# Attention scores with the keys on partitions, and row sums by a product with ones, in an attention and GRU kernel

## The chip, the core and the metric

The kernel runs on one core of one Trainium2 chip. The metric is the device time of one execution in microseconds (us). Engines: TensorE (PE, whose weight loads are listed apart as PEld), VectorE (DVE), ScalarE (ACT), GpSimd (POOL), and SyncE (SP), which here issues nearly all transfers. Data that engines share lies in SBUF; PE writes to PSUM, which has 8 banks of 512 float32 numbers on each of 128 partitions.

## The reference

`x` is 16 batches of 256 rows of 512; 16 heads of 32; all float32. A first layer is attention, a second a GRU that walks the 256 rows of all batches together.

```
xn = rms_norm(x) * g_norm * (1 + scale) + shift          # scale, shift: cond @ W_emb + b_emb
q, k, v = split(xn @ W_qkv)                               # each 16 heads of 32
q, k = rms_norm(q) * g_q, rms_norm(k) * g_k               # over the 32 numbers of a head
attn = softmax(q @ k.T * 32 ** -0.5)                      # 256 x 256, for each head and batch
o = attn @ v
x = x + o + o @ W_out
# GRU over the 256 rows, h starts as cond
r, z = sigmoid(i_r + h_r), sigmoid(i_z + h_z)             # i = x_t @ W_ih + b_ih, h_ = h @ W_hh + b_hh
n = tanh(i_n + r * h_n);  h = (1 - z) * n + z * h
out[:, t] = x[:, t] + h
```

## The kernel before

**Stages.** The attention stage goes over the 16 batches and lasts until 666.6 us; the GRU's 256 steps follow, its first step at 672.7 us. Each engine has its own program, written out by hand, and they meet at semaphores (`wait_ge`, `then_inc`). The engines take their instructions in the order of the program.

**A pass.** The attention stage has 64 passes, p = 0 to 63, four to a batch (b = p // 4, v = p % 4). A pass handles 8 heads for 128 queries. `scores(p + 1)` (L572) makes eight products of 32 x 128 by 32 x 256 with the queries on the output's partitions, in four row groups at a time. `maxima` (DVE, L872) takes the row maxima, negated, in two reductions of 1024 numbers for each partition. `exps` (ACT, L1237) takes eight exponentials of 256 numbers with the maximum as bias and collects the row sums beside them. `turn_p` (PE, L591) turns the probabilities, eight 128 x 128 transposes for each half of the pass; `keep_turned_p` copies them out of PSUM, half on ACT (L1252) and half on DVE (L887). `times_v` (L606) multiplies by v, sixteen products with 32 output rows and 128 columns. `recips` and `turn_recips` (L976, L980, L614) turn the row sums' reciprocals, `scale` (L892) applies them, `high` and `low` split the result in a rounded part and a rest for the output product.

**Filling.** Between these stand the large products, each of twelve 128 x 128 by 128 x 512 instructions (x and weights each split in a rounded part and a rest, three terms): six `project` products for a batch's q, k and v (L512) and two `out_proj` products (L627). The function `slots(p)` says which stands where: two in each pass. Piece `("project", b, i, g)` is rows 128 i to 128 i + 127 of batch b, g = 0 for q, 1 for k, 2 for v.

**Preparing q and k.** Each q or k product is copied to SBUF (`keep_raw`), squared (`square_raw`), both on ACT, summed by heads (`squares`, DVE L820), raised to the power -0.5 on POOL (`rsqrt`, L1427 and L1431) and multiplied (`normalize`, DVE L827). k and the second half of q then go out to DRAM and back in another layout, and DVE turns them in 32 x 32 blocks (`turn_k` L837, `turn_q` L846); the first half of q is turned on PE (`turn`, L551) inside a large product. `scale_q` (ACT, L1223) applies g_q, g_k and the scale. For the batch after, x is loaded in blocks; `square_blocks` (ACT, L1153), `x_sums` (DVE, L792), `sums` (PE, L705), `x_mean` (DVE) and `scale_blocks` (POOL, L1411 and L1414) norm it; `turn_x`, `affine` (DVE, L803, L811), `x_high` (ACT, L1164) and `x_low` (POOL, L1422) make the operands of its products.

## Time and profile before

| | |
|---|---|
| median of 3 runs | 1676.29 us (1675.59 to 1678.32) |
| the profiled execution | 1676.52 us, of it the span of the trace 1674.7 us |
| attention stage, by its last `times_v` | until 666.6 us |
| first GRU step on PE | 672.7 us |
| one batch of the attention stage (middle) | 39.84 us |
| PE busy in 294 to 372 us | 78.00 of 78.00 us |
| DVE, ACT, POOL busy there | 63.64, 59.27, 35.99 us |

In the rows below, a matmul in float32 is listed as two instructions and one in float32r (a rounded float32) as one; a transpose is one.

### The profile page before, as it was taken

How to read it: one execution, taken by the hardware profiler on the slowest of the kernel's cores; microseconds unless marked ns; L12 is line 12 of the kernel's file. 1: busy time of each engine (PE TensorE's matmuls, PEld its weight loads, DVE VectorE, ACT ScalarE, POOL GpSimd, SP SyncE). 2: the span in 40 equal slices, each digit the busy share in tenths (PEclk: the TensorE clock that was granted, in tenths of full speed). 3: DMA queues.
4: the chain of work that ended last, by engine and by line, in shares of the span. 5: the costliest groups of instructions: out<-in, count | busy, mean ns of one | idle time of the engine just before them, and what ended most of it. 6: DMA issues, size and time to landing. Idle time of an engine off the chain costs nothing.

```text
span 1674.7 us, 71812 instructions
## 1 busy us (share of the span) xinstructions
PE 1658.6 (99%) x30549; PEld 1292.1 (77%) x30549; DVE 1194.5 (71%) x4267; ACT 933.4 (56%) x3139; POOL 409.3 (24%) x464
## 2 busy tenths in 40 slices
PE   9999999999999999999999999999999999999998
PEld 7787777888788887777777777777777777777776
DVE  6888878888888876666666666666666666666665
ACT  5777777777777776444444444444444444444443
POOL 4544444444444430011111111111111111111111
PEclk9999999999999999999999999999999999999999
DMA  6244443333344426211111111111111111111110
GB/s 202 57 118 124 115 100 89 89 96 96 96 97 102 94 76 149 44 30 25 31 30 27 28 30 27 30 29 27 32 28 27 32 29 26 32 29 26 31 25 16
DMA packets 234280, 100.02 MB, mean 60 GB/s; under 512 B 141196, under 2 KB 213720, under 8 KB 233960
## 3 DMA queue, kind: packets, MB, share of 16 engines
q1 hardware_dynamic: 233840, 95.40, 23.0%
q8 instruction: 240, 3.93, 1.0%
q14 instruction: 80, 0.66, 0.1%
q10 hardware_dynamic: 120, 0.04, 0.0%
HBM read 58.38 MB, written 36.96 MB: 57 GB/s over the span
## 4 chain that ended last, share of the span: by engine, by line
PE 95%; DVE 1%; ACT 1%; POOL 1%; SPq 1%; issue 1%; DMA 1%; DVEq 0%; ACTq 0%; POOLq 0%
PE ps L763 40%; PE ps L649 20%; PE ps L512 14%; PE ps L591 7%; PE ps L627 5%; PE ps L572 4%; PE ps L606 3%; PE ps L614 1%; POOL rq L1431 1%; SPq L285 0%; PE ps L551 0%; ACT P L1237 0%; PE ps L533 0%; DVE nmx L872 0%; PE ps L541 0%
## 5 line engine op out<-in xcount | busy, mean ns | idle before, releaser
L649 PE MATMUL ps<-wih,x1T 128*32 128x192 f32 x8192 | 379.6, 326 | 0.3 <-issue 0.3
L1373 ACT ACTIVATE v<-ps 128x128 f32<-128x128 f32 x512 | 140.7, 275 | 414.6 <-PE ps L763 414.6
L763 PE MATMUL ps<-whh,hTE 128*32 128x192 f32 x8192 | 356.3, 326 | 1.1 <-DVE hTE L1102 1.1
L763 PE MATMUL ps<-whh,hTO 128*32 128x192 f32 x8192 | 356.3, 326 | 0.0
L1486 POOL TENSOR_TENSOR outG<-hG,x1g 128x128 f32<-128x128 f32 x255 | 116.3, 456 | 920.4 <-DVE hG L1095 920.4
L649 PEld LDWEIGHTS ps<-wih,x1T 128*32 128x32 f32 x8192 | 266.5, 110 | 66.7 <-issue 0.6
L763 PEld LDWEIGHTS ps<-whh,hTE 128*32 128x32 f32 x8192 | 249.8, 110 | 84.3 <-DVE hTE L1102 15.5
L763 PEld LDWEIGHTS ps<-whh,hTO 128*32 128x32 f32 x8192 | 250.0, 110 | 83.0 <-issue 0.4
L1075 DVE SCALAR_TENSOR_TENSOR v<-v,ps 128x64 f32<-128x64 f32 x512 | 113.4, 222 | 237.5 <-ACT v L1373 237.5
L1237 ACT ACTIVATE P<-ps,nmx 128x256 f32<-128x256 f32 x496 | 229.7, 483 | 0.3 <-DVE nmx L872 0.3
L1381 ACT ACTIVATE v<-v 128x64 f32<-128x64 f32 x512 | 131.5, 257 | 132.5 <-DVE v L1080 132.5
L1431 POOL TENSOR_TENSOR rq<-msq,mh 128x16 f32<-128x16 f32 x64 | 185.9, 2905 | 5.3
L872 DVE TENSOR_REDUCE nmx<-ps 128x4 f32<-128x1024 f32 x128 | 156.0, 1219 | 18.1 <-PE ps L572 18.0
L1091 DVE TENSOR_TENSOR v<-v,v 128x64 f32<-128x64 f32 x512 | 115.7, 226 | 63.6 <-ACT v L1381 48.1
L512 PE MATMUL ps<-wqh,xh 128*128 128x512 f32 x360 | 151.5, 421 | 1.5 <-ACT xt L1192 1.5
L512 PE MATMUL ps<-wql,xh 128*128 128x512 f32 x360 | 141.6, 393 | 0.0
L1377 ACT ACTIVATE v<-v 128x64 f32<-128x64 f32 x512 | 131.6, 257 | 16.1
L512 PE MATMUL ps<-wqh,xl 128*128 128x512 f32 x360 | 140.5, 390 | 0.0
L591 PE MATMUL ps<-ident,P 128*128 128x128 f32 x1024 | 138.5, 277 | 1.0 <-DVE rTs L892 0.7
L591 PEld LDWEIGHTS ps<-ident,P 128*128 128x128 f32 x1024 | 114.1, 142 | 30.7 <-issue 20.8
L1252 ACT COPY PT<-ps 128x512 f32<-128x512 f32 x128 | 74.3, 581 | 92.9 <-PE ps L591 92.9
L1095 DVE SCALAR_TENSOR_TENSOR hG<-v,v 128x64 f32<-128x64 f32 x512 | 114.3, 223 | 8.8
(139 smaller groups left out, 2155.5 us busy)
## 6 DMA issues: line engine op xcount, KB each, us to landing
xres<-in_x_dram SPq DMA_DIRECT2D x32, 256.0 KB, 3.4
...
xblk<-x1s SPq DMA_DIRECT2D x128, 64.0 KB, 2.7
x1g<-xscr SPq DMA_DIRECT2D x128, 64.0 KB, 2.0
...
```

The source lines that it names most:

```text
L512: last = pe.matmul(pB, xp[e2][:, c, m], wp[:, c, n], start=(k == 0), stop=(k == 3 * KC - 1))
L591: last = pe.transpose(pP[:, j, k, :], P[:, U % 4, j, 128 * k:128 * k + 128], ident)
L649: last = pe.matmul(gb[pr % 2][q][32 * j:32 * j + 32, 64:256], x1T[:, tt % 2, r, c, :], wig[:, c, :, 128 * j + 64 * q:128 * j + 64 * q + 64 ...
L763: last = pe.matmul(gb[e][q][32 * j:32 * j + 32, 0:192], h[:, c, :], whg[:, c, :, 128 * j + 64 * q:128 * j + 64 * q + 64], start=False, sto ...
L872: done = v.tensor_reduce(nmx[:, p % 2, j, :], ps[:, j, :].rearrange("p j (e t) -> p j e t", e=2), AXX, ALU.max, negate=True)
L1091: v.tensor_tensor(v_n[:, q, :], v_n[:, q, :], v_c[:, q, :], ALU.mult).then_inc(s_d, 1)
L1237: last = s.activation(P[:, (2 * p + e) % 4, j, :], pS[e][:, j, :], ACT.Exp, scale=rq0[:, 4 * (2 * p + e) + j:4 * (2 * p + e) + j + 1] if p ...
L1373: s.activation(v_rz[:, q, :], gb[e][q][:, 64:192], ACT.Tanh, scale=0.5).then_inc(s_tr, 1)
L1377: s.activation(v_c[:, q, :], v_rz[:, q, 64:128], ACT.Copy, bias=0.5, scale=-0.5)
L1381: s.activation(v_n[:, q, :], v_w[:, q, :], ACT.Tanh).then_inc(s_n, 1)
L1431: g_.tensor_tensor(rq0 if k == 2 else rq[:, i, :], msq[:, i, :], mh, ALU.pow).then_inc(s_rq, 1)
L1486: g_.tensor_tensor(outG[:, tt % 2, k, :], hG[:, t % 2, :], x1g[tt % 2][:, k // 2, :], ALU.add).then_inc(s_og, 1)
```

## The change

A pass becomes a group G, again 64, four to a batch (w = G % 4), but of four heads for all 256 queries. In the diff and in what follows, n = b + 1 and m = b + 2.

- Rounded copies of q and k (`qTr`, `kTr`, float32r) are made once for a batch by two new copies of 1024 numbers on ACT (`round_q`, `round_k`). `first_scores` makes the scores of these copies with queries on partitions, only to take the row maxima.
- The maxima are turned on PE (`turn_maxima`, two transposes), copied out on ACT (`keep_maxima`), and brought into the real scores by a product with a 0/1 matrix (`SEL`, four instructions of 512 columns). The real `scores` have the keys on partitions and are added to it in the same PSUM banks 0 to 3.
- `exps` is now two exponentials of 1024 numbers without bias or sums, and its output needs no turning: `turn_p` and `keep_turned_p` go (16 transposes, two copies on ACT and two on DVE for each pass).
- Row sums: DVE adds the two key tiles (`add_tiles`, two of 512 numbers), PE multiplies the sum by ones (`row_sums`), DVE turns, inverts and turns back (`recips`, 256 and 8 and 256 numbers) and scales.
- `high` moves from DVE to ACT, `low` from DVE to POOL.
- `slots(G)` puts the large products in another order, `turn_maxima(G + 1)` inside the first of a group's two, behind 8 of its 12 instructions. The q turn stands within the second one of w = 1, likewise.
- At the start, q of batch 0 is normed and turned in full before the first scores. The second half of `wih` is loaded only near the end of the attention stage, since its place is taken until then.

```
+def slots(G):
...
+    if w == 3:
+        return [("project", m, 0, 1), ("project", m, 1, 1)] if m < NB else [None, None]
+    if w == 0 and n < NB:
+        return [("project", n, 1, 0), ("project", n, 0, 0)]
+    if w == 1 and n < NB:
+        return [("project", n, 0, 2), ("project", n, 1, 2)]
+    if b and w == (2 if n < NB else 0):
+        return [("out", b - 1, 0), ("out", b - 1, 1)]
+    return [None, None]
+def within(G):
+    b, w = G // 4, G % 4
+    return ("turn", b + 1, 0, 0) if w == 1 and b + 1 < NB else None
+def behind(G):
+    b, w = G // 4, G % 4
+    return ("sums", b + 2) if w == 0 and b + 2 < NB else None
+PASS = {5: [], 6: [("project", 0, 1, 0)], 7: [("rows", 1, 0)]}
+for _G in range(-1, NP):
+    for _k, _x in enumerate(slots(_G)):
+        if _x:
+            PASS[6 + _k].append(_x)
+    PASS[5] += [_x for _x in (("maxima", _G + 1) if _G + 1 < NP else None, behind(_G), within(_G)) if _x]
+for _i in range(2):
+    PASS[6 + _i].append(("out", NB - 1, _i))
...
+            load_x1()
+            sp.wait_ge(s_S1, NP)
+            emptied(sp, ("out", NB - 2, 1))
+            load_wih(1)
...
+                    if k == 8 and between:
...
+            def first_scores(G):
+                b, c = G // 4, G % 4
+                if c == 0:
+                    pe.wait_ge(s_qr, 2 * b + 2)
+                if G:
+                    pe.wait_ge(s_ex, 2 * G)
+                for i in range(2):
                     for j in range(4):
                         q = slice(32 * j, 32 * j + 32)
...
+                        last = pe.matmul(ps[:, j, 256 * i:256 * i + 256], qTr[q, i, c, :], kTr[q, c, :], start=True, stop=True)
+                last.then_inc(s_S1, 1)
+            def turn_maxima(G):
+                bank_free(("maxima", G))
+                pe.wait_ge(s_mx, 2 * G + 2)
+                for i in range(2):
+                    last = pe.transpose(ps[:, 5, 128 * i:128 * i + 128], nmx[:, i, :], ident)
+                last.then_inc(s_nT, 1)
+            def scores(G):
+                b, c = G // 4, G % 4
+                emptied(pe, ("maxima", G))
+                if G == 0:
+                    pe.wait_ge(s_sel, 3)
+                for j in range(4):
+                    q = slice(32 * j, 32 * j + 32)
+                    pe.matmul(ps[:, j, :], SEL[q, :], nmT[q, :].unsqueeze(1).to_broadcast([32, 2, 256]), start=True, stop=False,
+                              skip_group_check=True)
+                for k in range(2):
+                    for j in range(4):
+                        q = slice(32 * j, 32 * j + 32)
+                        last = pe.matmul(ps[:, j, 256 * k:256 * k + 256], kT[b % 2][q, c, 128 * k:128 * k + 128], qT[b % 2][q, :, c, :],
+                                         start=False, stop=(k == 1), skip_group_check=True)
...
+                for k in range(2):
+                    for j in range(4):
+                        h = 4 * c + j
+                        pe.matmul(pO[32 * j:32 * j + 32, :], V[:, b % 2, k, 32 * h:32 * h + 32], PT[:, G % 2, k, j, :],
+                                  start=(k == 0), stop=(k == 1))
+            def row_sums(G):
+                pe.wait_ge(s_ps, 2 * G + 2)
+                for j in range(4):
+                    last = pe.matmul(pR[32 * j:32 * j + 32, :], ones, PS[:, j, :], start=True, stop=True)
...
-            def turn_recips(p):
-                bank_free(("recips", p))
-                pe.wait_ge(s_rb, p + 1)
-                for e in range(2):
-                    last = pe.transpose(pR[:, 128 * e:128 * e + 128], rB[:, e, :], ident)
-                last.then_inc(s_rT, 1)
...
+            def group(G):
+                first, second = slots(G)
+                if G + 1 < NP:
+                    first_scores(G + 1)
+                if G >= 0:
+                    times_v(G)
+                    row_sums(G)
+                fill(first, (lambda: turn_maxima(G + 1)) if G + 1 < NP else None)
+                if G + 1 < NP:
+                    scores(G + 1)
+                if behind(G):
+                    passed(behind(G))
+                inner = within(G)
+                fill(second, inner and (lambda: passed(inner)))
+            for G in range(-1, NP):
...
+                    v.wait_ge(s_sel, 3)
+                v.tensor_reduce(nm4[:, j, :], ps[:, j, :].rearrange("p j (i t) -> p j i t", i=2), AXX, ALU.max,
+                                negate=True).then_inc(s_mx, 1)
+            def add_tiles(G, h):
+                j = slice(2 * h, 2 * h + 2)
+                v.wait_ge(s_ex, 2 * G + h + 1)
+                if G:
+                    v.wait_ge(s_pv, G)
+                v.tensor_tensor(PS[:, j, :], PT[:, G % 2, 0, j, :], PT[:, G % 2, 1, j, :], ALU.add).then_inc(s_ps, 1)
+            def recips(G):
+                v.wait_ge(s_pv, G + 1)
+                v.transpose(rA, pR).then_inc(s_rt, 1)
+                v.wait_ge(s_rt, G + 1)
+                v.reciprocal(rinv, rA.rearrange("p (u k) -> p u k", k=32)[:, :, 0]).then_inc(s_ri, 1)
+                if G >= 2:
+                    v.wait_ge(s_ol, G - 1)
+                v.wait_ge(s_ri, G + 1)
...
+                add_tiles(G, 0)
+                add_tiles(G, 1)
+                if G + 1 < NP:
+                    maxima(G + 1, 0)
+                    maxima(G + 1, 1)
+                if w == 0 and n < NB:
...
+                    normalize(n, 0, 1)
+                elif w == 1 and n < NB:
+                    squares(n, 0, 0)
+                    normalize(n, 1, 0)
+                elif w == 3 and b and n < NB:
+                    out_sum(b - 1, 1)
+                recips(G)
+                scale(G)
+                if w == 0 and n < NB:
+                    if m < NB:
+                        x_sums(m)
                     normalize(n, 1, 1)
...
+                    squares(n, 1, 0)
+                    if m < NB:
+                        x_mean(m)
+                elif w == 1 and n < NB:
+                    normalize(n, 0, 0)
                     turn_k(n)
...
+                    if m < NB:
+                        turn_x(m)
+                        affine(m, 0)
+                elif w == 2 and n < NB:
+                    if m < NB:
+                        affine(m, 1)
+                    turn_q(n)
+                    if b:
...
+            def round_q(n):
+                if n:
+                    s.wait_ge(s_q1, n)
+                    emptied(s, ("turn", n, 0, 0))
+                    s.wait_ge(s_S1, 4 * n)
+                else:
+                    s.wait_ge(s_qk0[0], 2)
+                s.copy(qTr, qT[n % 2]).then_inc(s_qr, 1)
+            def keep_maxima(G):
+                s.wait_ge(s_nT, G + 1)
+                s.copy(nmT, ps[:, 5, 0:256]).then_inc(s_ev[5], 1)
+            def exps(G, h):
+                j = slice(2 * h, 2 * h + 2)
+                s.wait_ge(s_S, G + 1)
+                if G >= 2:
+                    s.wait_ge(s_pv, G - 1)
+                s.activation(PT[:, G % 2, :, j, :], ps[:, j, :].rearrange("p j (k t) -> p k j t", k=2), ACT.Exp).then_inc(s_ex, 1)
+            def high(G):
...
+                keep(slots(G - 1)[1])
+                if G:
+                    high(G - 1)
                 if w == 0 and m < NB:
                     square_blocks(m)
...
+                if w == 2 and n < NB:
+                    keep_turned_q(n, 0)
+                    scale_q(n)
+                    round_q(n)
+                    if m < NB:
+                        x_high(m, 0)
+                if G + 1 < NP:
+                    keep_maxima(G + 1)
+                keep(slots(G)[0])
+                if w == 2 and n < NB:
+                    round_k(n)
+                    if m < NB:
                         x_high(m, 1)
...
+                if G + 1 < NP:
+                    exps(G + 1, 0)
+                    exps(G + 1, 1)
...
+            def low(G):
+                b, c = G // 4, G % 4
+                e = (b + 1) % 2
+                g_.wait_ge(s_oh, G + 1)
+                g_.tensor_tensor(ol[e][:, c, :], oS[:, G % 2, :], oh[e][:, c, :].bitcast(F32), ALU.subtract).then_inc(s_ol, 1)
...
+                if G:
+                    low(G - 1)
+                if w == 0 and n < NB:
+                    rsqrt(n, 1, 1)
+                    rsqrt(n, 1, 0)
+                    if m < NB:
+                        scale_blocks(m)
+                elif w == 1 and n < NB:
+                    rsqrt(n, 0, 0)
+                elif w == 2 and m < NB:
                     x_low(m, 0)
                     x_low(m, 1)
+                elif w == 3 and m < NB:
+                    rsqrt(m, 0, 1)
```

On PE this is one group (w = 1) now, from `first_scores` to `scores`, with the last third of the first large product between:

```order
L561 MATMUL ps<-kTr,qTr 128x256 x8
L601 MATMUL ps<-PT,V 32x256 x8
L608 MATMUL ps<-PS,ones 32x256 x4
...
L512 MATMUL ps<-wqh,xl_90 128x512
L568 MATMUL ps<-ident,nmx 128x128 x2
L512 MATMUL ps<-wql,xh_88 128x512
...
L579 MATMUL ps<-nmT,SEL 128x512 x4
L584 MATMUL ps<-qT_84,kT_86 128x256 x8
L512 MATMUL ps<-wqh,xh_88 128x512
```

The scores' products L584 now stand behind the maxima of the same group, and no transposes of P are left.

On ACT, at the end of a pass with v = 0 in the kernel before: `scale_q` (L1223, its input turned by DVE) stood behind the exponentials (L1237).

```order
L1237 ACTIVATE P,rsum<-ps,nmx 128x256 x4
L1192 COPY xt<-ps 128x4x4x32
L1211 ACTIVATE sq<-xt 128x512
L1252 COPY PT<-ps 128x512
L1237 ACTIVATE P,rsum<-ps,nmx 128x256 x4
L1223 ACTIVATE qT_85<-xt,gqs 128x512
L1192 COPY xt<-ps 128x4x4x32
```

On ACT now, a group with w = 2, between the exponentials of one group and of the next (both L1218):

```order
L1218 ACTIVATE PT<-ps 128x2x512 x2
L1188 COPY V<-ps 128x512
L1225 CAST oh<-oS 128x256
L1175 ACTIVATE qT_83<-ps,gqs 128x512
L1180 ACTIVATE qT_83<-kx,gqs 128x512
L1207 CAST qTr<-qT_83 128x1024
L1122 CAST xh_89<-xf 128x512
L1211 CAST nmT<-ps 128x256
L1197 CAST kTr<-kT_85 128x1024
L1122 CAST xh_89<-xf_105 128x512
L1218 ACTIVATE PT<-ps 128x2x512 x2
```

`scale_q` (L1180), `round_q` (L1207) and `x_high` (L1122) now stand ahead of `keep_maxima` (L1211), and on DVE `turn_q` (L843), which `scale_q` waits for, stands in the same group behind `maxima`, `recips`, `scale` and `affine`.

On POOL in the kernel before, from a batch's second `rsqrt` (two instructions each) over `scale_blocks` (L1411, L1414) to its third:

```order
L1427 TENSOR_SCALAR msq<-ssq 128x16
L1431 TENSOR_TENSOR rq<-msq,mh 128x16
L1411 TENSOR_TENSOR rxp<-msp,mh 128x8
L1414 TENSOR_TENSOR xb<-xb,rxp 128x1024
L1427 TENSOR_SCALAR msq<-ssq 128x16
L1431 TENSOR_TENSOR rq<-msq,mh 128x16
```

On POOL now, from the last `rsqrt` of w = 0 (L1400, L1404) to the one of w = 1:

```order
L1400 TENSOR_SCALAR msq<-ssq 128x16
L1404 TENSOR_TENSOR rq<-msq,mh 128x16
L1383 TENSOR_TENSOR rxp<-msp,mh 128x8
L1386 TENSOR_TENSOR xb<-xb,rxp 128x1024
L1410 TENSOR_TENSOR ol_82<-oS,oh_73 128x256
L1400 TENSOR_SCALAR msq<-ssq 128x16
L1404 TENSOR_TENSOR rq<-msq,mh 128x16
```

The `rsqrt` ahead of `scale_blocks` was that of k's second half; now it is that of q's second half, whose product stands in the same group, and `low` (L1410) has come between.

## Rows read from the trace of the kernel before

**Rows 1.** The page's parts 1 and 2: busy us by engine; the clock granted to PE.
```profile
PE 1658.6 (99%) x30549; PEld 1292.1 (77%) x30549; DVE 1194.5 (71%) x4267; ACT 933.4 (56%) x3139; POOL 409.3 (24%) x464
...
PEclk9999999999999999999999999999999999999999
```
**Rows 2.** Busy us (and instructions) of PE, PEld, DVE, ACT, POOL, clock, DMA.
```profile
294.00:372.00 78.00, 78.00 (x721) 62.39 (x719) 63.64 (x110) 59.27 (x181) 35.99 (x23) 1.00 0.39 96
```
**Rows 3.** The chain that ended last, in order of time: start us, us, what.
```profile
290.35 1.01 PE ps L606 x32
...
320.39 1.01 PE ps L606 x32
321.40 1.08 PE ps L572 x16
322.48 1.02 PE ps L591 x8
...
323.72 2.77 PE ps L512 x12
326.49 0.87 PE ps L591 x8
327.36 2.82 PE ps L512 x12
330.19 1.01 PE ps L606 x32
```
**Rows 4.** The same chain where the GRU begins.
```profile
661.23 3.65 DMA x1n<-x1s
...
672.67 2.74 PE ps L763 x64
```
**Rows 5.** DVE's instructions in order of time: start us, us, what, [idle before <-releaser].
```profile
312.74 1.23 DVE L872 TENSOR_REDUCE nmx<-ps 128x4 f32<-128x1024 f32 x1 [0.58 <-PE ps L572]
313.88 0.68 DVE L887 COPY PT<-ps 128x512 f32<-128x512 f32 x1
314.48 0.68 DVE L827 TENSOR_TENSOR raw<-raw,rq 128x512 f32<-128x512 f32 x1
315.08 1.22 DVE L872 TENSOR_REDUCE nmx<-ps 128x4 f32<-128x1024 f32 x1
```
**Rows 6.** DVE groups by line: count, busy us, mean ns of one, idle before.
```profile
L846 DVE STREAM_TRANSPOSE xt<-raw 128x512 f32<-128x512 f32 x15 | 10.6, 706 | 2.7 <-DMA raw<-qscr 2.7
L892 DVE TENSOR_TENSOR rTs<-ps,rTs 128x256 f32<-128x256 f32 x64 | 26.9, 420 | 16.5 <-PE ps L606 16.5
L811 DVE TENSOR_SCALAR xf<-xt,Aff,Shf 128x256 f32<-128x256 f32 x56 | 20.4, 407 | 0.0
L976 DVE RECIPROCAL rinv<-rsum 128x8 f32<-128x8 f32 x64 | 12.4, 193 | 37.8 <-ACT P L1237 37.8
```
**Rows 7.** ACT groups by line, the same columns.
```profile
L1237 ACT ACTIVATE P<-ps,nmx 128x256 f32<-128x256 f32 x496 | 229.7, 483 | 0.3 <-DVE nmx L872 0.3
...
L1246 ACT COPY rTs<-ps 128x256 f32<-128x256 f32 x64 | 23.9, 373 | 5.6 <-PE ps L614 1.5
L1164 ACT CAST xh<-xf 128x512 fp32r<-128x512 f32 x30 | 18.9, 633 | 10.1 <-DVE xf L811 10.1
L1153 ACT ACTIVATE sqx<-xb 128x1024 f32<-128x1024 f32 x14 | 14.9, 1065 | 12.3 <-DMA xb<-in_x_dram 12.3
L1223 ACT ACTIVATE qT<-xt,gqs 128x512 f32<-128x512 f32 x15 | 11.1, 743 | 0.0
```
**Rows 8.** POOL groups by line, the same columns.
```profile
L1431 POOL TENSOR_TENSOR rq<-msq,mh 128x16 f32<-128x16 f32 x64 | 185.9, 2905 | 5.3
L1422 POOL TENSOR_TENSOR xl<-xf,xh 128x512 fp32r<-128x512 f32 x29 | 37.0, 1277 | 95.6 <-ACT xh L1164 86.9 <-ACT xh L1168 8.7
L1414 POOL TENSOR_TENSOR xb<-xb,rxp 128x1024 f32<-128x1024 f32 x14 | 26.7, 1909 | 1.1
L1411 POOL TENSOR_TENSOR rxp<-msp,mh 128x8 f32<-128x8 f32 x14 | 22.9, 1637 | 21.9 <-DVE msp L798 21.9
```
**Rows 9.** PE's instructions in order of time at the start, the first two scores.
```profile
31.51 1.15 PE L572 MATMUL ps<-kT,qT 32*128 32x256 f32 x16 [0.78 <-DVE kT L831]
...
39.44 1.15 PE L572 MATMUL ps<-kT,qT 32*128 32x256 f32 x16
```
**Rows 10.** DMA issues: engine, kind, count, KB each, median us to landing.
```profile
wih<-in_L_cond_W_ih_dram SPq DMA_DIRECT2D x3, 1024.0 KB, 6.0
```

606 lines of the change are left out of this document (209 added, 397 removed).

## The prediction, made before the changed kernel was run

> **What bounds the kernel now.** I read the page's busy shares first: PE is busy 99% of the span and the clock granted to it is full in every slice [rows 1]. The GRU stage is not touched but for its start, so the attention stage is read alone: in 78 us of its middle PE is busy for all 78.00 us, DVE for 63.64 [rows 2]. Then the chain that ended last: it runs on PE without a gap, one pass from 320.39 to 330.19 us, four passes from 290.35 to 330.19, which is 39.84 us for a batch [rows 3]. A pass is bound by the work on PE: work taken from PE is gained in full, as long as PE still never waits. So there are two questions: how much PE work is left, and whether the new order makes it wait.
>
> **PE's work.** Of a pass go the transposes of P, 1.02 + 0.87 us, those of the reciprocals (about 0.2, what is left of 9.80 after the other rows), and `times_v` in its old shape, 1.01 [rows 3]. What comes:
> - `first_scores`: eight instructions. The old scores, 16 instructions, took 1.08 us, 0.067 each [rows 3]; so 0.54. Bounds: 0.27, if one pass over the columns in float32r is half of a float32 instruction's; 0.87, if they follow each other like the eight transposes [rows 3]. The value taken is that of the same shape.
> - `turn_maxima`: two transposes, a quarter of 0.87, 0.22.
> - the selector product: four instructions of 512 columns. Twelve such take 2.77, 0.23 each [rows 3], so 0.92 one after another, 0.23 if four row groups run at a time as in the scores; taken 0.28.
> - the real scores: 1.08 as before, the same shape.
> - `times_v` and `row_sums`: 16 and 8 instructions with 32 output rows and 256 columns. The GRU's, with 192 columns, take 2.74 for 64, 0.043 each [rows 4], so 0.057 here: 0.91 and 0.46.
> - two large products, 2.81 and 2.80.
>
> A group is 9.10 us. With the q turn (four transposes, 0.44) and `sums` (0.1) a batch is 37.0 us against 39.84: **PE has 2.9 us less work for each batch**, if it never waits. Bounds of the unknown ones together: 8.8 to 10.1 for a group.
>
> **The chain through a group.** Now I follow the waits, since four engines hand to each other: `first_scores(G + 1)` needs the banks that the exponentials of G read, `maxima` follow, `turn_maxima`, `keep_maxima` on ACT, the scores, the exponentials. Durations for the others: on DVE the next instruction starts 1.14 us after a reduction of 1024 numbers and 0.60 after an operation on 512, DVE starts 0.06 behind PE [rows 5]; so two maxima are 2.36. `recips` and `scale`: a turn of 512 is 0.71, an operation on 256 is 0.42 [rows 6]; I take 0.44 for each turn of 256, 0.19 for the reciprocal, 0.42 for `scale`, 0.1 at each of three waits in between, in all 1.7. On ACT [rows 7]: 0.37 for `keep_maxima` and `high`; 1.06 for a copy of 1024; 0.63 for 512; 0.74 for `scale_q`; exponentials of 1024: 0.48 for 256 plus 768 further at the slope of the two copies (0.26 for 256) make 1.25, against 1.06 for a square; I take 1.1, 2.15 for both. On POOL [rows 8]: an `rsqrt` 2.9 + 0.3, `scale_blocks` 1.64 + 1.91, `low` half of 1.28.
>
> Times in each group from its first instruction on PE:
> - *w = 3.* `first_scores` to 0.54, maxima 0.60 to 2.96; PE has `times_v`, `row_sums` and eight instructions of the large product until 3.79, turns the maxima until 4.01; `keep_maxima` until 4.43, under the rest of the product (4.94). Scores to 6.30, exponentials to 8.5, second product to 9.10. PE never waits: 9.1 us.
> - *w = 0.* DVE goes on from 2.9 with `squares`, `normalize` (0.6 each) and `recips`, `scale` to 5.8, then `x_sums` to 6.95. `sums` on PE stands ahead of the second product and waits for it, from 6.30 to 7.1: 10.0 us. DVE then norms k's second half and sums q's second half (8.2). Its `rsqrt` ends at 11.5, `scale_blocks` at 15.1, both on POOL.
> - *w = 1*, from 10.0. POOL is busy with that until 5.1, `low` until 5.8, and only then takes the `rsqrt` of q's first half: 9.05. `normalize` ends at 9.75. The q turn on PE, in the second product, would be due at 8.2: it starts at 9.9, and the group takes 11.3 us. Behind it DVE has `turn_k`, `turn_x` (as a reduction of 1024, 1.16 each), two `affine` (0.41 each), so 12.8, and the next `add_tiles` 14.0, 2.7 us into the next group.
> - *w = 2*, from 11.3. `row_sums` wait for that (3.3), the maxima end at 5.1. DVE: `recips`, `scale` 6.7, `affine` 7.4, `turn_q` 8.1. ACT has waited for `turn_q`: `scale_q` 8.9, `round_q` 10.0, `x_high` 10.6, and only then `keep_maxima` 10.9. **PE, done at 6.4, waits 4.6 us for the maxima.** Scores to 12.35, second product to 15.15 (exponentials 14.65, since `round_k` and `x_high` stand ahead of them): 15.15 us.
>
> Together 45.55 us for a batch, 5.7 more than before. What is queued behind ACT's wait for `turn_q` is thus the one copy that PE needs; in the kernel before, `scale_q` stood behind the exponentials.
>
> **The rest.** Start: the first scores ran at 31.5 us and the first pass began at 39.4 [rows 9]. Now q's second half has to be squared, normed (3.2 on POOL), turned (0.44 and 0.69 of copy) and rounded (1.06) before them; by the same durations the first scores run at 42 and group 0 begins near 50.6. End: batch 14 has fewer products and no `x_sums` (38.0 us for it), three groups of batch 15 follow (24.1). Then the last group, two output products one after the other, the transfer of the last rows (3.65 [rows 4]), the second half of `wih` (1.5 MB, where 1 MB lands in 6.0 us [rows 10], queued behind SP's other issues): 18.3, bounds 15 to 21. GRU's first step: 50.6 + 14 x 45.55 - 0.5 (no output product in batch 0) + 38.0 + 24.1 + 18.3 = 768.2, against 672.7 [rows 4]: 95.5 later. The sum stands against the profiled execution, 1676.5 us, which is within 0.3 of the median of the runs. **Forecast 1772 us.** SP's transfers of q and k come early enough by this sum (k is stored in w = 0 and used in w = 1 at 9.8 us; q stored in w = 1, used in w = 2), so they add nothing; x in blocks has a batch's time.
>
> **Rivals.**
> 1. *Only the q chain.* If POOL is quicker to get to q's first half, no delay is carried into w = 2. Even then, in w = 2 everything from 2.96 on stands in one chain: 1.7 + 0.75 + 0.7 + 0.8 + 1.05 + 0.6 + 0.4 + scores 1.35 + product 2.8, so 13.1 us; 9.1 + 9.6 + 9.6 + 13.1 = 41.4 a batch, 14 x 4.15 less: 1714. For it: `rsqrt` would only have to come 1.7 us sooner. Against: it must wait for `squares` at 8.2 and the three POOL operations between are rows of the trace.
> 2. *PE's clock falls.* In no row of the kernel before does PE stand idle for long, and the granted clock is full in all [rows 1]. A wait of 4.6 us in each batch is new. If the clock goes from 2.4 to 1.2 GHz there, the scores and the product behind it (1.35 + 2.8) take twice as long: 13 x 4.15 = 54 more, 1826. The Trainium skill (TensorE: Matmul & The Clock Gate, "HAM oscillation — how this bites in real kernels") says that PE kept waiting between bursts goes back to half the clock and starts the next burst slow; by that rule the sum would be 1826, no row of this kernel shows it.
> 3. *The other side: PE stays the bound.* If `turn_q` to `x_high` were done by 4.0 us after a group's start, PE would have 37.0 us a batch and nothing else: 14 x 8.55 less, 1652, faster. It decides at 4 us of chain; the durations are those of the same instructions in the trace, and the order of instructions on ACT and DVE is fixed, so this asks for errors of half of all of them.
> 4. *Something between 1 and 3*, some 1680: shorter turns on DVE and all of PE's unknowns at their lower ends.
>
> **How the numbers follow.** Forecast 0.60, rival 1 0.19, rival 2 0.10, rival 3 0.06, rival 4 0.05. A measurement tells 0.2%, 3.4 us, from no change. Rival 3 is faster; of rival 4 I put 0.02 to faster and 0.02 to the same, of the rest 0.01 to the same: faster 0.08, same 0.03, slower 0.89. The range goes from below rival 1 to between the forecast and rival 2, which takes in the bounds of PE's unknowns (-4 to +14 x 4 x 0.5 where PE is not waiting anyway): 1705 to 1812; it leaves out rivals 3 and 4 and half of rival 2 or so.
>
> **What would show it.** Right: in the waits of the changed kernel, PE's scores (the selector product) wait for ACT's `nmT` some 4 to 5 us once in a batch, ACT's `scale_q` waits for DVE's `turn_q`, the q turn on PE waits for DVE some 1 to 2 us; a batch takes 45 to 46 us; DVE's `normalize` of q waits for POOL. Wrong: PE busy all the time again; the selector product or `first_scores` several times as long as taken; a wait that ends on a transfer; a granted clock below 1.

## Result: 1822 us, 8.7% slower than the kernel before, and 10 us past the range

| | before | after |
|---|---|---|
| median | 1676.2 us | 1822.0 us (1820.5 to 1823.2) |
| ratio | 1 | 1.087 (95% interval 1.085 to 1.089) |
| profiled execution, its span | 1676.5, 1674.7 us | 1822.6, 1820.7 us |
| first GRU step on PE | 672.7 us | 818.6 us |
| one batch in the middle | 39.84 us | 46.9 to 49.8 us |

The forecast was 1772 us with a range of 1705 to 1812. The direction and the places of the waits were as foreseen, the size fell short by 50 us. All of the loss lies ahead of the GRU: its first step is 145.9 us later, and the stage itself takes as long as before. The page of the changed kernel, its busy times, the granted clock and the shares of the chain that ended last:

```profile
PE 1674.1 (92%) x29781; PEld 1165.4 (64%) x29781; DVE 1190.8 (65%) x4200; ACT 799.8 (44%) x2211; POOL 479.7 (26%) x531
...
PEclk9889999999999999989999999999999999999999
...
PE 69%; POOL 13%; DVE 9%; issue 5%; ACT 3%; DMA 1%; SPq 0%; DVEq 0%; POOLq 0%; ACTq 0%
```

PE was busy 99% of the span [rows 1]; now it is 92%. Its busy time rose by 15.5 us although there is less work, since part of it ran at a lower clock: the clock row has 8s in it. The chain, all PE in a batch before [rows 3], now goes through POOL for 13% of the span. Who waited for whom in the attention stage (60 to 800 us), each row with the sum, the number of times and the longest:

```profile
ACT qT L1180 <- DVE kx L843: 96.2, 15, 6.7
...
DVE raw L827 <- POOL rq L1404: 60.9, 15, 4.4
...
PE ps L579 <- ACT nmT L1211: 52.9, 18, 4.7
...
PE ps L548 <- DVE raw L827: 32.5, 14, 2.4
...
PE ps L608 <- DVE PS L880: 20.1, 13, 1.7
...
PE ps L706 <- DVE ssp L790: 7.2, 13, 0.6
```

The four rows of PE are the four waits of the prediction: the selector product (L579) on the copy of the maxima, the turn of q (L548) on DVE's `normalize`, the row sums (L608) on `add_tiles`, `sums` (L706) on `x_sums`. No row of PE ends on a transfer in the middle of the stage. By the starts of `first_scores` the groups of a batch are, in us:

| group | predicted | after, batches 0 to 13 | over the prediction, 14 batches |
|---|---|---|---|
| w = 0 | 10.0 | 10.1 | 1.8 |
| w = 1 | 11.3 | 12.25 to 12.31; 13.4 and 13.1 in the first two | 15.6 |
| w = 2 | 15.15 | 15.2 in four, 16.5 to 16.8 in eight, 18.1 in two | 19.0 |
| w = 3 | 9.1 | 9.3; 12.2 in the first | 5.8 |

With the start (1.4 us later than taken) and batches 14, 15 and the tail (86.7 us where 80.4 were taken) this is the 50 us.

**The third group (w = 2)** on ACT, columns start, duration, engine, line, output and input; it begins at 318.18 us:

```profile
326.50 0.72 ACT L1180 ACTIVATE qT<-kx,gqs 128x512 f32<-128x512 f32 x1 [6.73 <-DVE kx L843]
327.25 1.04 ACT L1207 CAST qTr<-qT 128x1024 fp32r<-128x1024 f32 x1
328.20 0.61 ACT L1122 CAST xh<-xf 128x512 fp32r<-128x512 f32 x1
328.72 0.36 ACT L1211 CAST nmT<-ps 128x256 fp32r<-128x256 f32 x1
```

and on PE in the same stretch, large products left out:

```profile
323.91 0.38 PE L568 MATMUL ps<-ident,nmx 128*128 128x128 f32 x2
...
329.14 0.80 PE L579 MATMUL ps<-nmT,SEL 32*128 32x512 f32 x4 [3.92 <-ACT nmT L1211]
329.73 1.49 PE L584 MATMUL ps<-qT,kT 32*128 32x256 f32 x12
```

The maxima were turned at 324.3, and their copy (L1211) ended at 329.1, 10.9 us into the group, which is the prediction's figure: ACT stood 6.73 us ahead of `scale_q`, waiting for `turn_q`, with the copy behind it. What the sum did not have is the next view, the same place in windows of 3 us (PE, PE's weight loads, DVE, ACT and POOL busy, then the granted clock):

```profile
326.00:329.00 3.00, 0.00 (x0) 0.00 (x0) 1.04 (x2) 2.47 (x5) 0.10 (x1) 1.00 0.58 136
329.00:332.00 3.00, 2.86 (x21) 1.96 (x22) 0.00 (x0) 1.83 (x4) 2.44 (x2) 0.53 0.76 160
332.00:335.00 3.00, 3.00 (x16) 2.14 (x15) 1.39 (x2) 1.96 (x3) 0.96 (x1) 0.90 0.00 0
335.00:338.00 3.00, 3.00 (x38) 1.93 (x38) 2.48 (x3) 0.00 (x0) 0.00 (x0) 1.00 0.02 5
```

PE does nothing for 3 us, and the granted clock then is 0.53, about the lower level of 1.2 GHz, 0.90, and full again. That is rival 2, in part: four instructions of the selector product take 0.80 us (0.50 at the full clock), the third group 16.8 us instead of 15.2.

The groups of 15.2 us are not those where the clock held. In batch 6, whose third group begins at 366.68, the same windows and the selector product read:

```profile
369.00:372.00 3.00, 2.11 (x11) 1.25 (x12) 3.00 (x4) 0.00 (x0) 0.00 (x0) 0.69 0.41 64
372.00:375.00 3.00, 3.00 (x12) 2.22 (x11) 2.80 (x8) 0.00 (x0) 0.00 (x0) 0.74 0.36 56
...
377.64 0.51 PE L579 MATMUL ps<-nmT,SEL 32*128 32x512 f32 x4 [2.38 <-ACT nmT L1211]
```

Here the clock fell sooner, behind the 1.70 us that PE had waited for the row sums, and was full again before the selector product. The first large product took longer by it, the wait for the copy shrank from 3.92 to 2.38 us, and the copy itself (L1211) began at the same place, 10.5 us into the group. The fall cost nothing. Batch 11 is the same, in batch 4 the fall stands behind the q turn of the group before, and in batch 0, whose group has no large products, the clock is low for most of the group. So the clock fell in all 14 batches; where it fell decided what it cost.

**The second group (w = 1)** begins at 305.93. On POOL:

```profile
304.35 0.65 POOL L1400 TENSOR_SCALAR msq<-ssq 128x16 f32<-128x16 f32 x1 [1.41 <-DVE ssq L818]
305.07 3.22 POOL L1404 TENSOR_TENSOR rq<-msq,mh 128x16 f32<-128x16 f32 x1
308.26 1.63 POOL L1383 TENSOR_TENSOR rxp<-msp,mh 128x8 f32<-128x8 f32 x1
309.97 1.90 POOL L1386 TENSOR_TENSOR xb<-xb,rxp 128x1024 f32<-128x1024 f32 x1
311.83 0.72 POOL L1410 TENSOR_TENSOR ol<-oS,oh 128x256 fp32r<-128x256 f32 x1
312.64 0.20 POOL L1400 TENSOR_SCALAR msq<-ssq 128x16 f32<-128x16 f32 x1
312.93 2.90 POOL L1404 TENSOR_TENSOR rq<-msq,mh 128x16 f32<-128x16 f32 x1
```

The last of these, the `rsqrt` of q's first half, ends at 315.83, 9.9 us into the group, where 9.05 was taken, and the turn of q follows it.

### The profile page after: what moved, and what is told of

Same layout as the page of the kernel before. It is cut to its first block, busy times and chain, and to the rows that moved or that the text cites. A ratio compares the mean times of both kernels' runs of the same rounds, so it can differ in the third digit from the quotient of the medians.

```text
span 1820.7 us, 69326 instructions
## 1 busy us (share of the span) xinstructions
PE 1674.1 (92%) x29781; PEld 1165.4 (64%) x29781; DVE 1190.8 (65%) x4200; ACT 799.8 (44%) x2211; POOL 479.7 (26%) x531
## 4 chain that ended last, share of the span: by engine, by line
PE 69%; POOL 13%; DVE 9%; issue 5%; ACT 3%; DMA 1%; SPq 0%; DVEq 0%; POOLq 0%; ACTq 0%
PE ps L761 36%; PE ps L643 18%; POOL rq L1404 8%; PE ps L512 5%; PE ps L621 3%; DVE nmx L871 2%; PE ps L584 2%; POOL xb L1386 1%; POOL msq L1400 1%; POOL ol L1410 1%; POOL rxp L1383 1%; DVE xf L809 1%; PE ps L601 1%; DVE PS L880 1%; DVE kT L837 1%
## 5 line engine op out<-in xcount | busy, mean ns | idle before, releaser
L643 PEld LDWEIGHTS ps<-wih,x1T 128*32 128x32 f32 x8192 | 246.3, 110 | 89.1 <-ACT ps L1332 1.4
L761 PEld LDWEIGHTS ps<-whh,hTE 128*32 128x32 f32 x8192 | 232.7, 110 | 101.4 <-DVE hTE L1060 21.7
L761 PEld LDWEIGHTS ps<-whh,hTO 128*32 128x32 f32 x8192 | 232.7, 110 | 100.1 <-DVE hTO L1060 20.2
L1033 DVE SCALAR_TENSOR_TENSOR v<-v,ps 128x64 f32<-128x64 f32 x512 | 113.7, 222 | 247.6 <-ACT v L1345 247.6
L1404 POOL TENSOR_TENSOR rq<-msq,mh 128x16 f32<-128x16 f32 x64 | 190.4, 2976 | 5.3
L871 DVE TENSOR_REDUCE nmx<-ps 128x4 f32<-128x1024 f32 x128 | 150.7, 1219 | 47.3 <-PE ps L561 47.2
L880 DVE TENSOR_TENSOR PS<-PT 128x512 f32<-128x512 f32 x128 | 86.8, 697 | 96.8 <-ACT PT L1218 96.5
L512 PE MATMUL ps<-wql,xh 128*128 128x512 f32 x360 | 147.9, 411 | 0.0
L1218 ACT ACTIVATE PT<-ps 128x1024 f32<-128x1024 f32 x128 | 124.3, 1023 | 32.9 <-PE ps L584 30.1
L1038 DVE SCALAR_TENSOR_TENSOR v<-v,ps 128x64 f32<-128x64 f32 x512 | 111.4, 218 | 8.8
L1043 DVE SCALAR_TENSOR_TENSOR v<-v,hs 128x64 f32<-128x64 f32 x512 | 102.2, 200 | 0.0
```

The lines of the kernel that those rows point to most:

```text
L512: last = pe.matmul(pB, xp[e2][:, c, m], wp[:, c, n], start=(k == 0), stop=(k == 3 * KC - 1))
L643: last = pe.matmul(gb[pr % 2][q][32 * j:32 * j + 32, 64:256], x1T[:, tt % 2, r, c, :], wig[:, c, :, 128 * j + 64 * q:128 * j + 64 * q + 64 ...
L761: last = pe.matmul(gb[e][q][32 * j:32 * j + 32, 0:192], h[:, c, :], whg[:, c, :, 128 * j + 64 * q:128 * j + 64 * q + 64], start=False, sto ...
L871: v.tensor_reduce(nm4[:, j, :], ps[:, j, :].rearrange("p j (i t) -> p j i t", i=2), AXX, ALU.max, negate=True).then_inc(s_mx, 1)
L1033: v.scalar_tensor_tensor(out=v_v[:, q, :], in0=v_rz[:, q, 0:64], scalar=1.0, in1=gb[e][q][:, 0:64], op0=ALU.add, op1=ALU.mult).then_inc(s_ ...
L1218: s.activation(PT[:, G % 2, :, j, :], ps[:, j, :].rearrange("p j (k t) -> p k j t", k=2), ACT.Exp).then_inc(s_ex, 1)
```

## The experiments

All times are medians; the kernel before had 1676.0 us beside them. The changed kernel (1822.0) is what the first four are told against.

**1. The copy of the maxima ahead.** On ACT only, in w = 2:

```
                     keep_turned_q(n, 0)
+                    keep_maxima(G + 1)
                     scale_q(n)
```

> On ACT alone, in the third group of a batch, keep_maxima stands right behind keep_turned_q, ahead of scale_q, round_q and x_high; nothing else moves. In the changed kernel PE has nothing to do from 325.1 to 329.1 us there (selector product L579 waits 3.9 us for nmT), scores follow at 329.7. Theory A (that copy alone holds PE): the third group falls from 16.5 us to 11.1 (its products end 2.8 us behind the scores), 13 x 5.4 = 70 us less: 1752. Theory B (the wait moves): scale_q, round_q, x_high, round_k and x_high still start when DVE's turn_q has ended (326.5) and take 4.0 us, the exponentials stand behind them and end at 332.4, and the first scores of the next group wait for those: third group 14.2 us, PE idle 3.1 us ahead of first_scores instead; 14 x 2.3 = 32 less, 1790, and if the granted clock falls in that wait as well 1808. Rival C: the clock's fall doesn't hang on this wait: same rows at half clock in the same place.

Measured: **1791.8 us**, ratio to the kernel before 1.068 (1.066 to 1.070). Theory B. ACT and PE in the third group of batch 2, which starts at 169.76:

```profile
175.91 0.37 ACT L1211 CAST nmT<-ps 128x256 fp32r<-128x256 f32 x1 [4.56 <-PE ps L568]
178.09 0.72 ACT L1180 ACTIVATE qT<-kx,gqs 128x512 f32<-128x512 f32 x1 [1.80 <-DVE kx L843]
```

```profile
183.85 0.51 PE L561 MATMUL ps<-kTr,qTr 32*128 32x256 f32 x8 [2.79 <-ACT PT L1218]
184.29 1.82 PE L601 MATMUL ps<-PT,V 128*32 128x256 f32 x16
```

The copy is 4.4 us earlier in the group (6.15 instead of 10.54), and PE has its scores at once. But `scale_q` still starts 8.3 us into the group, four more instructions of 0.6 to 1.05 us follow it, and only then the exponentials: the next `first_scores` wait 2.79 us for them. The wait went to the next place in the chain. Behind this wait the lower clock stands in eight of the first 14 batches, besides the first: `times_v` behind it takes 1.82 us instead of 1.07, and the fourth group 10.9 instead of 9.3 us in seven of them. The expectation had 1790 without any fall and 1808 with one in every batch; that the measured time lies within 2 us of the first is in part luck. In the trace the fourth groups are 1.0 us longer in the mean than in the changed kernel, which the 1790 left out; most of it came back where it left something out too, as the third groups are shorter by 2.75 us in the mean (2.3 expected) and batch 14 by 3.2. So taking away the longest wait of PE, 3.9 us in a batch, gained 2.2: 30 us over 14 batches.

**2. ACT's order changed further.** As before, with `round_k` ahead of the copy and the exponentials ahead of `scale_q`:

```
                     keep_turned_q(n, 0)
+                    round_k(n)
                 if G + 1 < NP:
                     keep_maxima(G + 1)
                 keep(slots(G)[0])
                 if G + 1 < NP:
                     exps(G + 1, 0)
                     exps(G + 1, 1)
+                if w == 2 and n < NB:
+                    scale_q(n)
+                    round_q(n)
+                    if m < NB:
+                        x_high(m, 0)
+                        x_high(m, 1)
```

> The changed kernel with ACT's order alone altered in the third group, further than moving the copy of the maxima: keep_turned_q, round_k, keep_maxima, exponentials, scale_q, round_q, x_high twice. POOL, DVE and PE as in the changed kernel. Theory A (what remains behind the copy is a chain on ACT): by the times of the run with the copy ahead (turn_q there ends 8.3 us into the group, the copy of the maxima at 6.5, scores start at 7.3) the exponentials run from 8.7 to 10.6 and round_q is done at 12.4, and the first scores of the next group follow there instead of at 13.7; the fourth group waits for the low parts, 10.4 as it is: 14 x 1.3 = 18 less than 1792: 1774. Rival B (the wait moves a third time, to the low parts on POOL, in full): 1788 to 1792.

Measured: **1773.1 us**, 1.057 (1.056 to 1.059). Theory A, within a microsecond. The third group takes 12.1 us (12.4 expected) in the six batches where the second takes its 12.25; in the other eight the clock falls behind the wait of the q turn and the second group takes 12.7 to 13.5 us, and in seven of these the third gives about as much back (10.5 to 11.3 us). The fourth takes 10.6 (10.4 expected), since it waits for the low parts of x. Two edits of ACT's order alone thus take back 49 of the 146 us.

**3. The `rsqrt` of q ahead on POOL.** On POOL only:

```
                     rsqrt(n, 1, 0)
-                    if m < NB:
-                        scale_blocks(m)
                 elif w == 1 and n < NB:
                     rsqrt(n, 0, 0)
+                    if m < NB:
+                        scale_blocks(m)
```

> On POOL alone, rsqrt of q's first half stands ahead of scale_blocks (which goes into the second group of the batch, behind it). In the changed kernel q's rsqrt (L1404) ends 9.9 us into that group, behind scale_blocks (1.63 + 1.90) and low; squares have been there since 3.5 us into the group. Theory A: the q turn's wait on PE (2.3 us of L548) is made by POOL's order. Then rq is there at 7.0, the turn at 7.9 waits for nothing, the second group is 10.2 us instead of 12.4: 14 x 2.2 = 31 less, 1791; the third group stays at 16.5, since turn_x (waiting for scale_blocks) keeps DVE as late as before against the group's start. Rival B: DVE's queue behind it is what counts (turn_x would now be the late one and the next row sums wait longer): second group 10.2, third group 18 or more, total within 10 us of 1822. Rival C: the time lies in PE's work (the group is long by its products): nothing changes.

Measured: **1795.5 us**, 1.071 (1.070 to 1.073). The second group is 9.77 us in every batch (10.2 expected): PE is never kept from turning q, as theory A has it. Of rival B a part is true as well. On POOL, then DVE, then PE, of batch 5, whose third group starts at 307.54:

```profile
302.01 2.90 POOL L1404 TENSOR_TENSOR rq<-msq,mh 128x16 f32<-128x16 f32 x1
304.88 1.64 POOL L1383 TENSOR_TENSOR rxp<-msp,mh 128x8 f32<-128x8 f32 x1
```

```profile
308.52 1.25 DVE L800 STREAM_TRANSPOSE xt<-xb 128x1024 f32<-128x1024 f32 x1 [1.73 <-POOL xb L1386]
```

```profile
311.79 1.08 PE L608 MATMUL ps<-PS,ones 128*32 128x256 f32 x8 [2.75 <-DVE PS L880]
```

`turn_x` is now what waits for POOL, and everything on DVE behind it, `add_tiles` first, is later against the group's start: the wait of the row sums grows from 1.70 to 2.75 us, and the third group from 16.6 to 17.1 in the mean. (Where the clock costs nothing it goes from 15.2 to 16.3, in six batches, by as much as the wait; the fall costs 1.6 us in the other eight.) The gain is 2.6 us in the second group, less 0.5 in the third.

**4. Work for PE in the wait.** Ahead of the selector product of w = 2, PE does 32 transposes that nobody reads. The expectation says batches 1 to 13; the condition in the code takes in batch 14 too, and the trace has 448 transposes there, 14 times 32:

```
+                if c == 3 and 1 <= b < NB - 1:
+                    bank_free(("out", b - 1, 1))
+                    warm(32, 7)
                 emptied(pe, ("maxima", G))
```

> PE does 32 transposes of the identity (128x128 each, into bank 7, which the next output product overwrites) ahead of its wait for the maxima in the third group, in batches 1 to 13. By 0.11 us each (eight took 0.87 in the kernel before) that is 3.5 us of the 4 us that PE waits; nothing that any engine waits for comes sooner. Theory A (the clock falls because PE stands still in this wait, and scores and product then run slow): granted clock 1.00 in the middle stages, scores back from 1.9 to 1.0 us, third group 15.2 us in every batch instead of 16.5: 13 x 1.35 = 18 less, 1804. Rival B (the slow rows have another cause: contention with ACT and DVE there): third group 16.5 as before, 1822. Rival C (the transposes delay the scores): over 1822, by up to 13 x 0.5 = 6.

Measured: **1802.5 us**, 1.076 (1.074 to 1.077). Theory A in the main: PE has more work, nothing comes sooner, and the kernel is 19.5 us faster. PE in batch 5, and the window of the scores:

```profile
319.19 3.66 PE L541 MATMUL ps<-ident 128*128 128x128 f32 x32
323.28 0.51 PE L582 MATMUL ps<-nmT,SEL 32*128 32x512 f32 x4 [0.44 <-ACT nmT L1214]
323.62 1.03 PE L587 MATMUL ps<-qT,kT 32*128 32x256 f32 x16
```

```profile
322.00:325.00 3.00, 2.56 (x30) 1.87 (x29) 0.00 (x0) 2.97 (x6) 1.51 (x2) 1.00 1.06 241
```

The wait that is left is 0.44 us, the granted clock stays 1.00 where it was 0.53, and the scores take 1.03 us. In none of batches 1 to 14 is the clock low behind the selector product. The third group takes 15.0 us in the mean of batches 1 to 13 instead of 16.6. What the theory had wrong is "1.00 in the middle stages" and "15.2 in every batch": the clock still falls in ten of batches 1 to 13, behind the waits of the q turn and of the row sums, which were not filled. Where it falls in the third group's first product, the transposes come too late, as rival C has it, and the group takes 16.3 us (four batches); where it falls at the end of the second group, that group takes up to 13.5 and the third 13.5 or 14.5. So 19.5 us is what filling one wait of a batch gives back net. It is the clock's, since PE has more work and no other engine less. It isn't a version to keep: it fills the wait that the next kernels remove.

**5. All in another order.** POOL as in experiment 3; on DVE `turn_x` and both `affine` behind `turn_q`; on ACT `round_k` ahead of the copy, `scale_q` and `round_q` behind it, the exponentials, then `x_high` twice; on PE the first product on x waits for the second half of the low part only at its third block of columns:

```
 elif w == 1 and n < NB:
     normalize(n, 0, 0)
     turn_k(n)
-    if m < NB:
-        turn_x(m)
-        affine(m, 0)
 elif w == 2 and n < NB:
-    if m < NB:
-        affine(m, 1)
     turn_q(n)
+    if m < NB:
+        turn_x(m)
+        affine(m, 0)
+        affine(m, 1)
```

> The changed kernel with the same work in another order. POOL: scale_blocks behind the rsqrt of q's first half. DVE: turn_x and both affine behind turn_q in the third group (they were ahead of it, one in the second group). ACT, third group: keep_turned_q, round_k, keep_maxima, scale_q, round_q, exponentials, x_high twice. PE: the first product on x waits for the low part's second half at its third block of columns. Theory A (order alone made the kernel slow; PE's work is 37 to 38 us a batch): turn_q ends 5.3 us into the third group, q is rounded by 6.4, PE waits for nothing over 1 us; groups 10.1, 10.2, 9.3, 9.3, a batch 38.9: 14 x 9.7 = 136 less, 1687. Theory B (the chain of the q turn is bound by the transfers through SP, which no row of a wait shows so far): turn_q waits for q's load, third group 11 to 12 us, 1715 to 1730. Rival C (PE bound in full, as the rival in the prediction): 37.0 a batch, 1652 to 1662.

Measured: **1705.9 us**, 1.018 (1.016 to 1.019), 19 us over theory A. A batch is 40.17 us in place of 38.9: 10.1, 9.8, 10.95, 9.3. The groups are as expected but for the third. There, POOL, DVE and PE:

```profile
316.16 1.90 POOL L1386 TENSOR_TENSOR xb<-xb,rxp 128x1024 f32<-128x1024 f32 x1
316.29 3.45 DVE L882 TENSOR_TENSOR PS<-PT 128x512 f32<-128x512 f32 x2
318.16 1.02 POOL L1410 TENSOR_TENSOR ol<-oS,oh 128x256 fp32r<-128x256 f32 x1
...
319.79 0.64 PE L610 MATMUL ps<-PS,ones 128*32 128x256 f32 x8 [1.20 <-DVE PS L882]
```

The two `add_tiles` take 3.45 us where they take 1.3 elsewhere. The first starts 0.13 us behind POOL's product of 1024 and takes 2.32 us, the second stands beside POOL's `low` (L1410) and takes 1.21; it is so in all 13 batches from 1 to 13, and each ends 0.55 us behind the instruction of POOL that was running. The row sums are late by it, and PE waits. None of the three theories had this. In this kernel single instructions of L882 go from 679 to 2320 ns, with a median of 693.

**6. The blocks' scaling later on POOL.** Out of the second group, into the third:

```
 rsqrt(n, 0, 0)
-    if m < NB:
-        scale_blocks(m)
 elif w == 2 and m < NB:
+    scale_blocks(m)
     x_low(m, 0)
```

> The reordered kernel of the run before, with POOL's scale_blocks (a power on 8 numbers, 1.6 us, and a product of 1024, 1.9 us) moved once more, from the second group's end into the third group, behind low. In the reordered kernel the two add_tiles at the start of the third group take 3.45 us (316.29) instead of 1.3, while POOL's product of 1024 runs (316.16 to 318.06); PE waits 1.2 to 1.7 us for the row sums there, and a batch takes 40.17 us. Theory A (the DVE instruction with two inputs in SBUF is held up while POOL's product runs): add_tiles take 1.3 us again, the third group 9.3 to 9.6 us instead of 10.95, a batch 38.6 to 38.8: 14 x 1.5 = 21 less, 1685. Rival B (add_tiles were slow for another reason: the transfers of x or ACT's copies at that time): 3.45 us and 1706 as before. Rival C (the product of 1024 now holds up maxima, recips or scale, or turn_x comes too late): third group 10 to 11 us, 1695 to 1706.

Measured: **1680.6 us**, 1.003 (1.002 to 1.004). Theory A, with 25 us where 21 were expected. DVE, and POOL in its new place:

```profile
305.56 1.25 DVE L882 TENSOR_TENSOR PS<-PT 128x512 f32<-128x512 f32 x2
...
309.84 1.90 POOL L1386 TENSOR_TENSOR xb<-xb,rxp 128x1024 f32<-128x1024 f32 x1
309.98 0.45 DVE L893 STREAM_TRANSPOSE oS<-rinv 128x256 f32<-128x256 f32 x1
310.46 0.42 DVE L897 TENSOR_TENSOR oS<-ps,oS 128x256 f32<-128x256 f32 x1
310.80 0.70 DVE L845 STREAM_TRANSPOSE kx<-raw 128x512 f32<-128x512 f32 x1
```

`add_tiles` are back at 1.25 us, none over 717 ns for one, and the third group at 9.33 us. Beside the same product of POOL, DVE's turn (0.45), its product with PSUM as one input (0.42) and the 512-number turn behind them (0.70) keep their usual times; what was held in experiment 5 reads two inputs from SBUF. That isn't the only kind: in the changed kernel `affine` (L809, one block of numbers and two columns from SBUF) takes 0.93 us in place of 0.41 eleven times, each with POOL's `low` beside it. Nor does every instruction of POOL hold them: 30 `add_tiles` of the changed kernel begin while POOL's power on 16 numbers runs (2.9 us) and take 0.69 to 0.72 us. The Trainium skill (SBUF — State Buffer, "SBUF: two separate sides") has this as a lock between DVE and GpSimd, held for a whole instruction, and names two SBUF inputs on DVE's side; by that rule the first `add_tiles` ends at 318.06 + 0.69 = 318.75 or so, 2.46 us after its start; the trace has 2.32, 0.14 less, which agrees in the main. The power on 16 numbers does not fit the rule as it stands.

**7. `sums` inside the second product.** As 6, and in w = 0 PE's small product for x stands behind eight of the twelve instructions of the second large product:

```
 def within(G):
     b, w = G // 4, G % 4
+    if w == 0 and b + 2 < NB:
+        return ("sums", b + 2)
     return ("turn", b + 1, 0, 0) if w == 1 and b + 1 < NB else None
 def behind(G):
-    b, w = G // 4, G % 4
-    return ("sums", b + 2) if w == 0 and b + 2 < NB else None
+    return None
```

> As the kernel with blocks later, and on PE the product sums stands inside the second large product of the first group, behind eight of its twelve instructions, instead of ahead of it. In all kernels so far that place costs 0.8 us in each batch (first group 10.13 us against 9.32 of the fourth, PE waits 0.55 us for ssp). Theory A (PE is then bound by its own work all through): first group 9.4, second 9.8, third and fourth 9.3 to 9.6, 37.8 to 38.1 us a batch; against the kernel with blocks later 14 x 0.75 = 10 less: 1675, if that one gives 1685. Rival B (sums comes too late for DVE and POOL: x_mean, then the rsqrt of q wait): second group 10.5 or more, no gain.

Measured: **1674.5 us**, 0.999 (0.998 to 1.000): the same as the kernel before. Theory A, with 6 us less than experiment 6 where 10 were expected; the batches give 0.56 us each instead of 0.75. A batch is 37.96 us: 9.55, 9.77, 9.34, 9.30. PE is bound by its own work again; its window, as [rows 2]:

```profile
294.00:372.00 78.00, 78.00 (x669) 53.49 (x670) 66.19 (x105) 44.86 (x69) 47.64 (x33) 1.00 0.40 97
```

**8. The tail.** As 7, with the output products of the last batch taken block by block as their inputs come, and the second half of `wih` issued ahead of the biases:

```
+                if G == NP - 2:
+                    for i in range(2):
+                        bank_free(("out", NB - 1, i))
+                        out_part(i, 0, 1)
...
-            for i in range(2):
-                passed(("out", NB - 1, i))
+            for i, c in ((0, 2), (1, 2), (0, 3), (1, 3)):
+                out_part(i, c)
```

> As the kernel with sums inside, and in the tail: the output products of the last batch start with their first two blocks of columns behind the last but one group's scores and go on block by block, instead of both whole behind the last group; SP issues the second half of wih ahead of the biases. In the reordered kernel the last low part is there at 683.0 us, the first output product's sum ends at 688.4, its rows land at 694.4 and the first GRU step starts at 701.1. Theory A (the tail is that chain): the product behind the last low part is 3 instructions, 0.7 us, for the first half of the rows instead of some 4.6: GRU starts 3.5 to 4 us sooner; 1671, if the kernel with sums inside gives 1675. Rival B (the transfers bound the tail: wih or x1 in blocks land no sooner): under 1 us of gain.

Measured: **1670.1 us**, 0.997 (0.996 to 0.998), which is 0.3% faster than the kernel before. Theory A; the first GRU step comes at 665.9 us, against 669.9 without this edit. The edit changes two things at once, the products' order and SP's; the rows below show the first at work, and what the second gave was not measured by itself. The end of it on PE and DVE, first without and then with the edit:

```profile
657.24 0.76 PE L624 MATMUL ps<-wo_h,oh 128*128 128x512 f32 x1 [3.15 <-POOL ol L1411]
...
662.46 0.69 DVE L910 TENSOR_TENSOR x1s<-ps,xres 128x512 f32<-128x512 f32 x1 [6.60 <-PE ps L624]
...
665.48 0.66 PE L632 MATMUL ps<-ident,x1n 128*128 128x128 f32 x4 [0.33 <-DMA x1n<-x1s]
```

```profile
655.06 0.51 PE L634 MATMUL ps<-wo_h,oh 128*128 128x512 f32 x1 [1.47 <-POOL ol L1426]
...
656.07 0.69 DVE L925 TENSOR_TENSOR x1s<-ps,xres 128x512 f32<-128x512 f32 x1 [2.30 <-PE ps L634]
...
658.88 0.75 PE L643 MATMUL ps<-ident,x1n 128*128 128x128 f32 x4 [2.15 <-DMA x1n<-x1s]
```

From the last low part to the sum of the first rows it is 1.0 us instead of 5.2. A part of the gain is lost again behind it: the products with `wih` (64 instructions) take 5.35 us, against 2.81 without the edit. PE now stands longer before them, and they run at the lower clock; the window:

```profile
661.00:664.00 3.00, 3.00 (x41) 1.77 (x37) 0.00 (x0) 0.26 (x1) 0.00 (x0) 0.50 0.45 130
```

## Why the prediction was right or wrong

**Right: what bounds the kernel and what the change does to it.** PE's work falls, and the order makes it wait. PE's work of a batch, 37.0 us by the prediction, is 37.96 in experiment 7, where PE never waits in the middle of the stage: 0.2 to 0.35 us over in each group, within the bounds (8.8 to 10.1 for a group). The terms one by one: `first_scores` 0.44 (0.54 taken), the selector product 0.34 (0.28), the scores 0.96 (1.08), `times_v` 0.88 (0.91), `row_sums` 0.55 (0.46), `turn_maxima` 0.14 (0.22); the two large products took 6.0 us (5.61 taken), since the first instruction behind another shape takes a step of 0.34 us instead of 0.23, which no term had. The exponentials took 1.94 us for the two (2.15 taken).

**Right: the third group's chain.** `scale_q` 8.3 us into the group (8.1 taken), the copy of the maxima at 10.5, the group 15.15 us: 15.2 in the four batches where the clock's fall cost nothing. Experiments 1 and 2 gave 1792 and 1773 us where the chain, followed on with the times of the trace, gave 1790 and 1774 (the first in part by luck, as said there).

**Wrong: the clock as an either-or (19 us in the third groups of batches 0 to 13).** The prediction held rival 2 apart, with a tenth of the chance, and priced it as everything behind the wait at half the clock, 4.15 us in each batch; in the sum itself the clock stood at nothing. The runs show both parts off. The clock fell in all 14 batches, so it belonged into the sum; and behind the selector product's wait the lower clock cost 1.3 to 1.6 us in eight, 2.9 in two and nothing in four, since it was full again well before the group's end (0.53, 0.90, 1.00 in three windows), and since in three of the four the fall came before the wait, which then took it up. Experiment 4 shows the cause: 19.5 us less when the wait is filled. The clock cost some 6 us more elsewhere: 1.9 in the second groups of the first two batches, 2.9 in the fourth group of the first, 1.6 in batch 14. It is the largest part of the miss. No row of the kernel before could give the price, only the sign; what could be seen was that PE would stand still for 4.6 us in each batch, which it had nowhere done. That deserved more than a tenth. The Trainium skill (TensorE: Matmul & The Clock Gate, "HAM oscillation — how this bites in real kernels") tells of a fall at every such wait, and the trace agrees in that it has one in each batch, though in three of 14 ahead of the long wait alone. That the sum by the rule, 1826, came within 4 us of the result is luck: its price for one fall was too high and the other terms were too low.

**Wrong: POOL's small instructions in w = 1 (16 us).** The step that failed is "`rsqrt` ends at 9.05". It ended at 9.9, so the 14 batches lose 1.0 us each. POOL began the `rsqrt` of q's second half 8.57 us into the group before (0.37 over the 8.2 taken), and it took 3.94 us with its two instructions of 0.65 and 3.22 (0.64 over the 3.3 between 8.2 and 11.5); the group before being 0.15 us longer, that makes the 0.85. Beside an idle DVE, at 312.64, the same two take 0.20 + 2.90. On DVE, just ahead of POOL's start at 304.35:

```profile
304.25 1.29 DVE L880 TENSOR_TENSOR PS<-PT 128x512 f32<-128x512 f32 x2
```

A two-input instruction from SBUF started 0.10 us earlier, and POOL's small one ends only behind the first of the two: what experiment 5 shows, seen from POOL. That this made the 0.64 us is read from rows only; no run took it away. That POOL's order makes the whole wait is shown (experiment 3: 9.77 us for the group). The rest is the clock: in the first two batches it is low from 11 us into the group on (0.50 in 73.5 to 75.5 us), and they take 13.4 and 13.1 us, 1.9 more together than the others.

**Wrong, smaller: start and end (11 us).** Group 0 began 1.4 us later than taken, and the fourth group of the first batch is 2.9 us longer than the others, with the clock low in its first 6.3 us; batch 14 takes 39.6 us (38.0 taken), since it has the clock's fall too; the three groups of batch 15 take 26.0 us (24.1 taken); the tail from the last `times_v` takes 21.0 us (18.3 taken, bounds 15 to 21), with the first output product at the lower clock: 0.43 us from one instruction to the next there, 0.23 in the second. The last 5 us are PE's own terms, 0.1 to 0.2 us in each first and fourth group.

**Rival 3, as a claim about the design, was right, and about this kernel wrong.** It asked for `round_q` to be done by some 4 us after the start of the third group, and put 1652 us to it. Order, not durations, was what stood against it: with the orders of experiments 5 to 8 the same work runs with PE bound, 37.96 us a batch against 39.84. The prediction said that this asks for errors of half of all durations; it took none, only another order. That it ends at 1670 and not at 1652 lies mostly in PE's work: the first GRU step comes 17 us behind that rival's sum, and 13.4 of them are 37.96 us a batch where 37.0 was taken, the rest a later start and a slower first batch. That it is only 6 us ahead of the kernel before has its reason in the two ends. If every batch before took 39.84 us from 39.4 on, the last batch and the tail took 35.6 us. In experiment 8 group 0 begins at 53.0 us, 13.5 later, and the last batch with the tail takes 43.5, 7.9 more; the batches between give back 28. A form that saves 1.9 us in each of 15 batches and pays 21 us once is worth 6 or 7.
